# Cross attention's key products, their casts and the first two query loads placed in the projection stage before it

## The reference, cut to what matters

```python
x = _layernorm(x + _L0_attn_ref(x, qkv_w, proj_w, proj_b, slopes))      # ends in: out @ proj_w.T + proj_b
x = _layernorm(x + _L0_xattn_ref(x, ctx, ctx, mask, Wq, bq, Wk, bk, Wv, bv, Wo, bo))

def _L0_xattn_ref(q, k, v, mask, ...):
    qh = _split_heads(q @ Wq.T + bq)
    kh = _split_heads(k @ Wk.T + bk)
    vh = _split_heads(v @ Wv.T + bv)
    scores = einsum('bhqd,bhkd->bhqk', qh, kh) / sqrt(16) + mask * NEG
    attn = einsum('bhqk,bhkd->bhqd', softmax(scores), vh)
    return attn.transpose(0, 2, 1, 3).reshape(B, L, 256) @ Wo.T + bo
```

## Time and profile before

| | us |
|---|---|
| median of 3 executions (lowest, highest) | 1902.18 (1900.19, 1906.13) |
| the profiled execution: its time | 1905.45 |
| its span in the trace | 1903.6 |
| share of the span that TensorE, VectorE, ScalarE, GpSimd are busy | 86%, 68%, 52%, 21% |
| projection stage: SyncE's first transfer is issued, first work after `const_in` | 933.24, 943.60 |
| cross stage: its first instruction, first scores | 1040.52, 1094.90 |
| router stage: SyncE's first transfer is issued | 1286.80 |

### The profile page before, as it was taken

The page is one execution under the profiler, slowest core; times in us unless marked ns, Lnnn a source line. Parts: engine busy times, 40 slices in busy tenths (PEclk is TensorE's granted clock), DMA queues, the critical chain, the costliest instruction groups (busy, mean ns, idle before and its releaser), DMA issues. The chain is left out here.

```text
span 1903.6 us, 36270 instructions
## 1 busy us (share of the span) xinstructions
PE 1637.1 (86%) x14816; PEld 1066.9 (56%) x14816; DVE 1302.4 (68%) x2288; ACT 993.9 (52%) x1692; POOL 403.4 (21%) x268
## 2 busy tenths in 40 slices
PE   7848999999999999999585699867993999999970
PEld 6724444444444444443274555545763888888870
DVE  6777888888888888884185637752333677777736
ACT  5323777777777777777434157853441333333310
POOL 6540000000000000000134200001552344444430
PEclk9956999999999999999788659988996999999995
DMA  7878454444544445410365858314213233333225
GB/s 254 194 181 236 59 67 66 68 68 64 69 63 70 64 66 67 64 29 9 120 198 184 116 75 135 79 48 137 90 40 109 67 92 92 92 92 92 37 32 178
DMA packets 131421, 183.98 MB, mean 97 GB/s; under 512 B 30918, under 2 KB 95572, under 8 KB 130200
## 3 DMA queue, kind: packets, MB, share of 16 engines
q1 hardware_dynamic: 117816, 159.60, 39.8%
q0 software_dynamic: 13440, 22.07, 5.4%
HBM read 114.99 MB, written 69.99 MB: 97 GB/s over the span
## 5 line engine op out<-in xcount | busy, mean ns | idle before, releaser
L638 DVE TENSOR_REDUCE att_row_max<-att_ring 128x2 f32<-128x1024 f32 x512 | 602.3, 1220 | 108.4 <-PE att_ring L704 56.9
L622 ACT ACTIVATE att_w_exp<-att_s_ps 128x512 f32<-128x512 f32 x1024 | 547.7, 596 | 232.3 <-PE att_s_ps L747 156.8
L774 PE MATMUL att_a_ps<-att_w_exp,att_v_group 128*32 128x512 f32 x2048 | 273.6, 606 | 0.2 <-ACT att_w_exp L622 0.2
L733 PE MATMUL att_s_ps<-att_q_stack,att_k_stack 62*128 62x512 f32 x640 | 181.5, 480 | 0.0
L733 PEld LDWEIGHTS att_s_ps<-att_q_stack,att_k_stack 62*128 62x128 f32 x640 | 84.4, 184 | 124.0 <-ACT att_w_exp L622 112.7
L2166 ACT ACTIVATE ex_hid<-ex_h_ps,ex_b 128x512 f32<-128x512 f32 x128 | 87.1, 685 | 118.0 <-DVE ex_h_lo L2221 64.8
L2122 POOL DMA_INDIRECT x_scr<-ex_y,ex_home x64 | 106.7, 1668 | 182.3 <-DVE ex_y L2211 167.6
L560 POOL COPY att_eyes<-keep_slope_eye 128x384 bf16<-128x384 bf16 x16 | 8.1, 507 | 641.5 <-PE att_s_ps L747 632.2
L2221 DVE TENSOR_TENSOR ex_h_lo<-ex_hid,ex_h_hi 128x512 fp32r<-128x512 f32 x128 | 138.8, 1085 | 4.4
L704 PE MATMUL att_ring<-att_k_stack,att_q_stack 60*128 60x512 f32 x640 | 131.3, 450 | 6.2 <-DVE att_att L665 3.2
L747 PE MATMUL att_s_ps<-att_eyes,keep_past_bf 64*128 64x64 bf16 x3840 | 133.1, 193 | 0.0
(11 more groups left out here) (291 smaller groups left out, 3550.1 us busy)
## 6 DMA issues: line engine op xcount, KB each, us to landing
first_w_raw<-ew SPq DMA_DIRECT2D x16, 1024.0 KB, 7.5
att_k_stack<-qk_scr SPq DMA_DIRECT2D x120, 128.0 KB
cr_q_stack<-q_scr SPq DMA_DIRECT2D x48, 256.0 KB, 9.4
keep_k_stack<-qk_scr SPq DMA_DIRECT2D x72, 128.0 KB
rows_scr<-att_zeros POOLq DMA_DIRECT2D x8, 1040.0 KB, 22.6
ex_rows<-rows_scr SPq DMA_DIRECT2D x16, 520.0 KB, 4.9
att_q_stack<-qk_scr SPq DMA_DIRECT2D x60, 128.0 KB
qk_scr<-qkv_t_hi SPq DMA_DIRECT2D x7, 1024.0 KB, 4.3
```

The lines of the kernel that those rows point to most:

```text
L622: nc.scalar.activation(w_exp[(STEPS * g.n + st) % SETS][h][:, :], s_ps[v % BANKS][:, :], ACT.Exp).then_inc(exp_done, 1)
L638: nc.vector.tensor_reduce(out, ring[place.slot][:, :, :], AX.X, ALU.max).then_inc(ring_free, 1)
L733: ins = nc.tensor.matmul(s_ps[v % BANKS][:, :], ks[g.buf][rows, c, j, kt * P:(kt + 1) * P], qs[g.buf][rows, j, c * CH:(c + 1) * CH], start ...
L774: ins = nc.tensor.matmul(a_ps[32 * h:32 * h + 32, :], vg[g.buf][:, kt, h * VW:h * VW + 32], w_exp[(STEPS * g.n + st) % SETS][h][:, :], sta ...
```

## The change

`load_cross` is issued in `stage_attention`, after the second group's stacks and ahead of `move_top(0)`; the tiles live from the program's start. It has 9 transfers now; `wo_raw` and `bo` are loaded in the projection stage. The identity of the first stage is kept instead of loaded again. All casts, the mask operations, the 8 key products and their `k_high`, `k_low`, `k_max`, `k_exp` are in `stage_self_out`: the casts ahead of the wait for `const_in`, products 0 to 3 after it on VectorE and ScalarE, products 4 to 7 between step 0's `split_att` and step 1. The query stacks 0 and 1 are filled by GpSimd there and loaded after the stores of steps 4 and 5. `att` and `x` have 4 buffers instead of 8, so that chunks 4 to 7 are loaded after residual 0 to 3, and GpSimd adds their bias between the norms. In `stage_cross` TensorE begins with all 14 halves of maxima, with the first shifts' transposes among them, and the value products come after. The shifts' way through HBM is issued by ScalarE: the store right after `copy_top`, the two loads two turns later (`send_top`), and ahead of the loop for chunk 0. `v_all` is filled by GpSimd, and `copy_top(0)` must be done before GpSimd's first bias.

```diff
@@ stage_attention, SyncE @@
             load_stacks(sp, io, Group.of(1), qs[1], ks[1], stack_in[1])
+            load_cross(sp, io, pre)
             move_top(sp, Group.of(0), 0, PLACES[None, "top", 0])
@@ load_query_stack, a function of its own now @@
+    for part, row in ((0, 0), (0, 16), (1, 32)):
+        for side in range(2):
+            src = io["q2_scr"][n, part].rearrange("k (j s d) t -> s d (k j) t", s=2, d=D)[side]
+            at = 64 * side + row
+            sp.dma_start(stack[at:at + D, :, :].bitcast(F32), src).then_inc(io["chunk_in"][n], 16)
@@ stage_self_out, SyncE @@
             def load(n):
+                if n >= LOADED:
+                    sp.wait_ge(t_done, n - LOADED + 1)
+                    sp.wait_ge(res_done, n - LOADED + 1)
...
-            for n in range(1, CHUNKS):
+            for n in range(1, LOADED):
                 load(n)
-            load_cross(sp, io, pre)
...
+                if n in (4, 5):
+                    sp.wait_ge(q_out[n - 4], 32)
+                    sp.wait_ge(stack_ready, n - 3)
+                    load_query_stack(sp, io, n - 4, stacks[n - 4])
@@ GpSimd @@
+            pool.memset(stacks[0][:, :, :].bitcast(F32), 1.0).then_inc(stack_ready, 1)
+            pool.wait_ge(const_in, 64)
+            for n in range(LOADED):
+                bias_x(n)
+            pool.wait_ge(k_done, PAIRS)
+            pool.memset(stacks[1][:, :, :].bitcast(F32), 1.0).then_inc(stack_ready, 1)
             for n in range(CHUNKS):
-                bias_x(n)
-            for n in range(CHUNKS):
                 pool.wait_ge(x1_done, min(n + 3, CHUNKS))
+                if n + LOADED < CHUNKS:
+                    bias_x(n + LOADED)
                 split_q(n)
@@ ScalarE @@
+            def key_high(j):
+                act.wait_ge(k_done, j + 1)
+                if j >= 2:
+                    act.wait_ge(k_step, 2 * j - 2)
+                nc.scalar.activation(k_high[j % 2][:, :], key_banks[j % KEY_BANKS], ...).then_inc(k_high_done, 1)
+                if j >= 2:
+                    key_exp(j - 2)
...
+            act.wait_ge(const_in, 64)
             nc.scalar.activation(w_hi[:, :, :, :], w_raw[:, :, :, :], ACT.Copy).then_inc(w_split, 1)
+            for j in range(KEY_BANKS):
+                key_high(j)
...
                     split_att(new)
+                if step == 0:
+                    for j in range(KEY_BANKS, PAIRS):
+                        key_high(j)
+                    for j in (PAIRS - 2, PAIRS - 1):
+                        key_exp(j)
@@ TensorE @@
+            def keys(j):
+                if j >= KEY_BANKS:
+                    pe.wait_ge(k_step, 2 * (j - KEY_BANKS) + 2)
...
+            pe.wait_ge(key_lo, 3)
+            for j in range(KEY_BANKS):
+                keys(j)
+            pe.wait_ge(const_in, 64)
@@ stage_cross, SyncE @@
-            load_stack(0)
-            load_stack(1)
             load_x(0)
             load_stack(2)
-            move_top(0)
...
-                if has(n + 1):
-                    move_top(n + 1)
@@ GpSimd @@
+            pool.memset(v_all[:, :, :, :], 0.0).then_inc(pool_done, 1)
+            pool.wait_ge(pool_done, 1)
+            pool.memset(v_all[:, :, :, D:D + 1], 1.0).then_inc(pool_done, 1)
+            for i in range(2, Q_SETS):
                 pool.memset(qst[i][:, :, :].bitcast(F32), 1.0).then_inc(pool_done, 1)
...
+            pool.wait_ge(top_copied, 1)
@@ ScalarE @@
+                act.wait_ge(top_copied, n + 1)
+                act.dma_start(io["shift_scr"][n % 2], neg_t[n % 2][:, :].bitcast(F32)).then_inc(top_out, 16)
+
+            def send_top(n):
+                act.wait_ge(top_out, 16 * n + 16)
+                for side in range(2):
+                    row = 64 * side + ROW_SHIFT
+                    act.dma_start(qst[n % Q_SETS][row:row + 2, :, :].bitcast(F32), ...).then_inc(top_in[n % 2], 16)
...
+                    if u == 4 and has(n + 1):
+                        send_top(n + 1)
@@ TensorE @@
-            pe.wait_ge(k_step, 2 * PAIRS)
-            for h in range(2):
+            for h in range(LEAD):
                 max_pairs(h)
-            pe.wait_ge(lo_done, 4)
+                if h == HALVES:
+                    transpose_top(0)
```

More of the change, by code:

```diff
@@ L1106, in _ @@
                     split_att(new)
+                if step == 0:
+                    for j in range(KEY_BANKS, PAIRS):
+                        key_parts(j)
                 if mid is not None:
@@ L1424, in _ @@
             copy_top(0)
-            act.wait_ge(prep, 5)
+            send_top(0)
             for n in range(CHUNKS + 2):
@@ L1538, in _ @@
             for h in range(LEAD):
-                if h == 2:
-                    for i in range(2):
-                        take_values(i)
                 maxima(h)
```

268 lines of the change are left out of this document (125 added, 143 removed).

## The result

The changed kernel is **slower**: 1938.74 us median of 6 executions (1929.53 to 1945.38), against 1904.16 of 6 of the kernel before (1897.31 to 1916.76). The ratio is 1.0181, 95% interval 1.0148 to 1.0214. I had forecast 1880, 22 us faster, and given "slower" a chance of 0.06.

What follows compares the result with a forecast made beforehand. The prologue was taken as latency, engines waiting for each other. Terms -31.4, -1.3, +5.1, +1.4, +2.5 and +1.7 sum to -22.0 us, taking the median from 1902.2 to 1880; own range 1873 to 1888, with two rivals 1865 to 1895.

Steps and rivals of the forecast that it cites:

- ScalarE's wait in `send_top`: Cross loop: ScalarE's three transfers and its wait for the shifts' store cost 0.2 us a chunk, +1.7 us.
- it becomes the bound: Rival, cross loop: ScalarE's wait for the store sets the pace; 34 us at 10.0 us landings, 1913; chance 0.05.
- L - 5.1 per chunk: Cross loop: a store landing in L us costs each of 7 chunks L less the 5.1 us before `send_top`.
- Cross prologue: Cross stage's first instruction to first scores: falls from 54.4 to 23 us, -31.4 us.
- T0: Time of the cross stage's first instruction, from which the prologue's times were counted; first scores forecast 23 us later.
- table load: Cross stage: a load of 1.28 us after the first scores moves ahead of the wait, -1.3 us.
- The first rival: Cross prologue: the shifts land with stacks 2 and 3, scores 11 us later, time 1891; chance 0.18.
- The loads of stacks 0 and 1 are hidden: Projection stage: issued after steps 4 and 5, three steps before the stage ends, these loads cost nothing.
- Projection stage, start and steps 3 to 6: Projection stage: key products at its start add 5.1 us, VectorE's variance waits in steps 3 to 6 add 1.4.
- Attention's start: Start of self attention: `load_cross` moves 1.09 MB through full DMA engines, +2.5 us, bounds 0 and 5.
- 9 issues of about 0.55 us end at 141.5: Attention's start: `load_cross` issues end before the shifts' store at 146.44, so issuing costs nothing.

Runs made afterwards that it cites:

- done-alone run: Kernel before the change, with only ScalarE's shifts added (store in `copy_top`, loads in `send_top`): 1940.03 us, ratio 1.0209.
- undone run: Changed kernel with the shifts' store and loads issued by SyncE again, as before the change: 1907.39 us, ratio 1.0025 to the kernel before.
- experiments 13 to 16: Nothing changed; experiment 9's kernel, experiment 5's, the kernel before and the changed kernel each profiled once more: 1884.96, 1892.42, 1906.68, 1942.78 us.
- experiment 10: As experiment 5, but query stacks 0 and 1 are loaded in the cross stage, ahead of `x` and the shifts: 1900.74 us, ratio 0.999.
- experiment 5: Changed kernel with the shifts on SyncE's queue and the cross loads issued late in self attention: 1896.99 us, ratio 0.9964 to the kernel before.
- experiment 9: As experiment 5, but the transfers of stacks 0 and 1 are issued three at a time after steps 3 to 6: 1886.94 us, ratio 0.9919.
- experiments 3 and 12: Changed kernel with ScalarE's shifts waited for and sent two turns later: 1930.93 us; the same with SyncE's stacks 2 and 3 held until the first shifts are in: 1920.75.
- experiment 1: Changed kernel with the cross loads issued in self attention's second to last window, not at its start: 1935.37 us, ratio 1.0152 to the kernel before.

## Why the prediction was wrong, point by point

*ScalarE's wait in `send_top`: the step that failed.* I put +1.7 us on it and gave "it becomes the bound" 0.05, at a landing of 8.3 us or more in every chunk. The profiled waits were 1.1 and 4.1 us in the loop, two chunks, so my rival's way of counting (L - 5.1 per chunk) would give 5 us, not 32. Missing was the second half: a wait that stops TensorE takes its clock away, and the loop's 32.1 us are half of the 65 us more that it spent at 1.2 GHz. The done-alone run (+37 us) and the undone run (-31 us) show the price of ScalarE's shifts, of which 24 and 33 us are the loop's in the profiles; the ten stops, one of them inserted, show the mechanism; and the later wait (loop 202.9 from 224.0) shows the place. Not all of the low clock follows a wait: 58 us of it do, and chance drops as in experiments 13 to 16 make up the rest of the excess. I had used the median of eight landings (5.9) for what is decided by the longest ones, and in the earlier trace rows I had read the low clock only at the loop's start. A rival of this name at 1913 stood in the prediction, but its sum, 34 us for landings of 10 us in all chunks, is near the measured 32 by luck: only one store after the first took over 4 us.

*Cross prologue, -31.4; measured -22.3.* Right in what was computed from instructions: shifts ready at T0 + 9.3, value products done at T0 + 20.3 (forecast 20.9), no waits for GpSimd, table load inside the wait. (TensorE's first idle of 18.3 us, which I read as the stage's, began 9.5 us ahead of its first instruction; no term used it.) Wrong in the landing, 11.7 and 9.4 us instead of 5.9 and 4.8. The first rival, "the shifts come behind the stack loads", had the cause and nearly the number (T0 + 34 forecast, 32.1 measured), the number by luck: it let the store land with the stacks, at T0 + 29, and took the way back at 4.8, while the store landed at T0 + 22.7 and the way back took 9.4. I gave it 0.18. With the stack loads held back the forecast's T0 + 23 comes out as 21.7. The Trainium skill ("DMA: Bandwidth & Descriptors", "Queues, rings and completion order") says that each DMA engine alternates between queues packet by packet. The trace agrees in so far as the store landed 8.4 us ahead of the last stack transfer issued before it. But I had read it as "lands sooner than in the row", and that the measurement refutes: 11.7 us on a queue of its own beside two stack loads, 9.1 behind one on the same queue, 1.66 alone. A queue of its own was no shortcut here.

*"The loads of stacks 0 and 1 are hidden."* A term put at nothing, and wrong by some 16 us (experiment 10). I had the price among the rivals: 3.1 MB of stack loads at 132 GB/s, 23 us of full DMA engines. I compared it with the time until the stacks are needed, not with the queue in front of `store_x1` and `store_q`, for which ScalarE waits within two steps.

*Projection stage, start and steps 3 to 6, +6.5.* The start was +4.6 (forecast 5.1), with the two waiting `k_max` as said. `so_var` took 0.28 to 0.30 us instead of 0.5, so steps 3 to 6 cost 0.5, not 1.4.

*Attention's start, +2.5.* Measured 8.3 in the profile, and 10.4 by medians (experiment 5), beyond my bound of 5. The failed step is "9 issues of about 0.55 us end at 141.5": the last ended at 156.4, and the shifts' store stood behind them.

*The size of the idea.* Much of the forecast gain of 22 us was there to be had. With the shifts on SyncE's queue, the cross loads late and the stack loads cut up (experiment 9) the change gives 18 us by medians and 15 by the ratio (0.9919).

## What to carry to other kernels

When a change moves transfers, write down for each queue what stands behind them and who waits for that, and count an issue at what a full row of transfers can make it (up to 6 to 9 us here), not at its idle price. Don't let an engine on TensorE's path wait for a transfer's landing: take the longest landing, not the median, and add the clock, since stops of 3.3 to 5.7 us were followed by 7 to 41 us at 1.2 GHz here. Large strided loads that could not be avoided were cheapest here in rows of three between the small stores.

## What the runs showed of the hardware that I had not expected

- After each of ten stops of 3.3 to 5.7 us TensorE was at 1.2 GHz, for 7 us in the shortest case and 41 in the longest, though it was busy nearly all of that time (34.76 of 36.00 us from 1214 to 1250).
- Gaps of 1.12, 0.45 and 0.56 us within 9 us sometimes bring the clock down and sometimes not, in the same kernel at the same place: 16.4 us of difference between two executions.
- A 64 KB store took 1.66 us alone and 11.7 us beside two stack loads on another queue, of which the last part landed 8.4 us after it.
- A transfer's issue, 0.4 us at the head of a row, took 6.3 and 8.7 us behind many others, and the shifts' store behind these issues left 10.0 us later.

What stays open: why the clock stays low as long as it does after a stop; whether the loops of 202.9 and 205.3 us with ScalarE's shifts but no wait (experiments 3 and 12) are chance, since SyncE's shifts gave 191 to 208; and why experiment 1 returned only 3.4 of its 9 us. The loop's chance drops would cover that, but no run shows it.
